# A perceiver layer on one core: the scores of the layer's own attention computed in two 64-row tiles of the TensorE array, with a PSUM bank for each

## The reference

```python
x = x + _L0_xattn_ref(_layernorm(x), ctx_1024, ctx_1024, ...)   # keys and values: 1601 rows a batch
x = x + _L0_attn_ref(_layernorm(x), ...)                        # the change is here
x = x + _L0_ffn_ref(_layernorm(x), ...)                         # 8 experts, the best 2 of a token

# _L0_attn_ref
qkv = jnp.einsum('bte,fe->btf', query, in_proj_weight).reshape(b, t, 3, H, D)
q = q / math.sqrt(D)
scores = jnp.einsum('bhqd,bhkd->bhqk', q, k)
scores = jnp.where(causal[None, None], scores, jnp.float32(-jnp.inf))
attn = jax.nn.softmax(scores, axis=-1)
out = jnp.einsum('bhqk,bhkd->bhqd', attn, v)
```

## Time and profile before

| | |
|---|---|
| median of 3 runs | 663.91 us (663.18 to 666.14) |
| profiled execution, its own time | 663.55 us |
| span of the profiled execution | 661.7 us |
| PE busy | 630.8 us, 95% |
| DVE busy | 475.3 us, 72% |
| ACT busy | 329.4 us, 50% |
| POOL busy | 301.9 us, 46% |
| chain that ended last | PE 74%, DVE 13% |
| mean granted TensorE clock | 0.989 |

### The profile page before, as it was taken

One profiled execution on the slowest core, in us unless ns is written; L12 is line 12 of the kernel. 1 busy time (PEld: TensorE's weight loads), 2 busy tenths in 40 slices (PEclk: granted clock), 3 DMA queues, 4 the chain that ended last, 5 costly groups with the idle time before them and its releaser, 6 DMA issues.

```text
span 661.7 us, 15583 instructions
## 1 busy us (share of the span) xinstructions
PE 630.8 (95%) x6304; PEld 532.8 (81%) x6312; DVE 475.3 (72%) x878; ACT 329.4 (50%) x541; POOL 301.9 (46%) x386
## 2 busy tenths in 40 slices
PE   7989999999989989989998999978989999999997
PEld 4778878868877868877887888757879999999997
DVE  4887757667687678688777868686777666656753
ACT  4355655555554555446555545463654444444421
POOL 2138788897686688678678768200000000000000
PEclk9999999999989999999999999998989999999999
DMA  6311110100010010011110000423003302330000
GB/s 184 134 50 52 28 51 26 51 27 26 27 52 1 27 50 27 26 27 51 27 27 26 2 1 2 152 106 127 1 1 128 128 26 104 127 127 0 0 0 33
DMA packets 13285, 34.11 MB, mean 52 GB/s; under 512 B 1563, under 2 KB 10532, under 8 KB 11044
## 3 DMA queue, kind: packets, MB, share of 16 engines
q1 hardware_dynamic: 13188, 33.19, 15.1%
q0 software_dynamic: 32, 0.01, 0.0%
HBM read 32.67 MB, written 0.52 MB: 50 GB/s over the span
## 4 chain that ended last, share of the span: by engine, by line
PE 74%; DVE 13%; issue 5%; ACT 3%; POOL 3%; DMA 2%; SPq 0%; POOLq 0%; DVEq 0%; ACTq 0%
PE bank L1207 46%; PE bank L1396 8%; PE bank L1216 7%; PE bank L1382 4%; PE bank L1277 3%; POOL prob_sum L490 3%; DVE maxes L923 3%; DVE ctx_lo L474 2%; DMA raw<-in_w 1%; ACT k_hi L626 1%; DVE k_lo L904 1%; PE bank L1332 1%; PE bank L1320 1%; PE bank L1304 1%; DVE prob_sum L490 1%
## 5 line engine op out<-in xcount | busy, mean ns | idle before, releaser
L490 POOL TENSOR_TENSOR prob_sum<-probs,prob_sum 128x256 f32<-128x256 f32 x336 | 270.6, 837 | 71.4 <-ACT probs L739 66.4
L739 ACT ACTIVATE probs<-bank 128x1024 f32<-128x1024 f32 (+1 forms) x104 | 106.6, 1025 | 111.6 <-PE bank L1396 99.2
L923 DVE TENSOR_REDUCE maxes<-bank 128x1 f32<-128x400 f32 (+1 forms) x256 | 129.5, 564 | 20.3 <-PE bank L1277 19.8
L721 ACT ACTIVATE h_raw<-bank,b_sb 128x512 f32<-128x512 f32 (+2 forms) x72 | 46.2, 642 | 106.5 <-PE bank L1207 106.3
L904 DVE SCALAR_TENSOR_TENSOR k_lo<-bank,bias_sb,k_hi 128x400 fp32r<-128x400 f32 (+2 forms) x64 | 40.5, 632 | 48.6 <-ACT k_hi L626 48.6
L1207 PE MATMUL bank<-w_hi,h_hi 128*128 128x256 f32 x256 | 73.6, 288 | 0.8 <-DVE h_lo L1142 0.8
L1207 PE MATMUL bank<-w_lo,h_hi 128*128 128x256 f32 x256 | 72.9, 285 | 0.0
L1207 PE MATMUL bank<-w_hi,h_lo 128*128 128x256 f32 x256 | 72.8, 284 | 0.0
L1216 PE MATMUL bank<-probs,v_sb 128*32 128x128 f32 (+1 forms) x1664 | 68.1, 282 | 1.0 <-ACT probs L739 0.5
L1141 DVE CAST h_hi<-h_raw 128x512 fp32r<-128x512 f32 (+2 forms) x72 | 28.5, 396 | 55.5 <-ACT h_raw L721 54.1
L1207 PE MATMUL bank<-wv_hi,ctx_hi 128*128 128x256 f32 (+1 forms) x208 | 65.3, 314 | 2.6 <-DVE maxes L923 2.4
(11 more groups left out here) (155 smaller groups left out, 1389.8 us busy)
## 6 DMA issues: line engine op xcount, KB each, us to landing
raw<-in_w SPq DMA_DIRECT2D x16, 1024.0 KB, 6.8
ctx_raw<-in_ctx_t SPq DMA_DIRECT2D x16, 400.0 KB, 3.6
ctx_raw<-in_ctx_t SPq DMA_DIRECT2D x8, 402.0 KB, 3.8
ctx_raw<-in_ctx_t SPq DMA_DIRECT2D x8, 399.0 KB, 3.6
w_sb<-in_w_t SPq DMA_DIRECT2D x1, 1280.0 KB
w_raw<-in_w_t SPq DMA_DIRECT2D x2, 256.0 KB, 4.7
result<-x_all SPq DMA_DIRECT2D x4, 128.0 KB, 2.0
x_all<-in_x SPq DMA_DIRECT2D x1, 384.0 KB, 4.1
```

Of the source, the lines that this page charges most:

```text
L490: ins = engine.tensor_tensor(prob_sum[0:ROWS[k], cols], probs[0:ROWS[k], s % 2, cols], acc[0:ROWS[k]], ALU.add)
L721: nc.scalar.activation(h_raw[:, c % 2, 0:width], bank[:, at, 0:width], ACT.Gelu, bias=b1_sb[:, bass.ds(e, 1), c:c + 1].rearrange("p a b -> ...
L739: nc.scalar.activation(probs[0:ROWS[k], s % 2, :].rearrange("p (g n) -> p g n", g=G), bank[0:ROWS[k], score_bank(b, k):score_bank(b, k) + ...
L923: nc.vector.tensor_reduce(maxes[:, g * PAIRS + j, c:c + 1], src[:, 0:width], AX.X, ALU.max).then_inc(read_dve, 1)
```

## The change

Own scores are computed in row tiles. Each of the 8 matmuls of `s0` and `s1` contracts over 64 rows in place of 128: the pairs of heads 0 and 1 of each group have their non-zero rows in rows 0 to 63, the pairs 2 and 3 in rows 64 to 127, so half of the 128 rows held zeros. Matmuls of the two row tiles alternate, and each row tile writes to a bank of its own. A piece `s0` is therefore two units, `("s0", 0)` and `("s0", 1)`; PE waits for both banks at once, then issues all 8 matmuls. DVE reads each bank with an instruction of its own, 256 elements a row in place of 512.

In a step these two units stand right behind the scores and the M units, ahead of K. In `CHAIN_AT` no K unit shares a step with `s0` or `s1`, so only step 7 of the last tile has another order. `GATE_BANKS` keeps `gt` and `b2` of the tail in the banks that they had, 3 and 6.

```diff
+GATE_BANKS = {"gt": 3, "b2": 6}
...
+        if banks is ALONE_BANKS:
+            for n, kind in enumerate(order):
+                self.bank[n] = GATE_BANKS.get(kind, self.bank[n])
...
-    others += [(c, 0) for c in chain]
-    row = m + others
+    others += [(c, 0) for c in chain if c not in ("s0", "s1")]
+    row = m + [(c, r) for c in chain if c in ("s0", "s1") for r in range(ROW_TILES)] + others
...
-                    nc.vector.tensor_tensor(soft[:, int(kind[1])], src.rearrange("p (n k) -> p n k", k=Q),
-                                            causal_sb[:, :].unsqueeze(1).broadcast_to([P, G * PAIRS, Q]),
+                    each = PAIRS // ROW_TILES
+                    nc.vector.tensor_tensor(soft[:, int(kind[1])].rearrange("p (g r i) q -> p r g i q", g=G, r=ROW_TILES)[:, u],
+                                            src[:, 0:G * each * Q].rearrange("p (g i q) -> p g i q", g=G, i=each),
+                                            causal_sb[:, :].unsqueeze(1).unsqueeze(1).broadcast_to([P, G, each, Q]),
...
-                    if kinds and kind not in kinds:
+                    if kinds and kind not in kinds or kind in ("s0", "s1") and u < ROW_TILES - 1:
...
-                    for g in range(G):
-                        for j in range(PAIRS):
-                            m = g * PAIRS + j
-                            ins = nc.tensor.matmul(dst[:, m * Q:m * Q + Q],
-                                                   own_queries[:, g, 2 * j:2 * j + 2, :].rearrange("p s q -> p (s q)"),
-                                                   k2_t[:, g, bi * Q:bi * Q + Q], start=True, stop=True)
+                    if u < ROW_TILES - 1:
+                        return
+                    each = PAIRS // ROW_TILES
+                    for g in range(G):
+                        for i in range(each):
+                            for r in range(ROW_TILES):
+                                rows, j = slice(RT * r, RT * r + RT), each * r + i
+                                at = (g * each + i) * Q
+                                ins = nc.tensor.matmul(bank[:, units.bank_of(n - ROW_TILES + 1 + r), at:at + Q],
+                                                       own_queries[rows, g, 2 * j:2 * j + 2, :].rearrange("p s q -> p (s q)"),
+                                                       k2_t[rows, g, bi * Q:bi * Q + Q], start=True, stop=True)
+                                if g == G - 1 and i == each - 1 and r < ROW_TILES - 1:
+                                    ins.then_inc(filled, 1)
```

More of the change, by code:

```diff
@@ L952, in after_units @@
             def after_units(units, s, *kinds):
-                for n, kind, _ in units.at[s]:
-                    if kinds and kind not in kinds:
+                for n, kind, u in units.at[s]:
+                    if kinds and kind not in kinds or kind in ("s0", "s1") and u < ROW_TILES - 1:
                         continue
@@ L1147, in alone @@
                     unit(TAIL, m, kind, u, TT - 1, B, 0)
-                    if kind == "s0":
+                    if kind == "s0" and u == ROW_TILES - 1:
                         after_units(TAIL, s, "s0")
```

## The result

The changed kernel takes 667.0 us (664.28 to 676.22, 20 executions), the kernel before on the same chip 663.23 us (659.46 to 671.58, 20 executions). The ratio is 1.0065 with a 95% interval of 1.004 to 1.009. Forecast were 662.7 us, a range of 661.0 to 666.2, and 0.84 for "no change": the time is outside the range, and it moved where no change was forecast. (Ratios here leave disturbed executions out, medians do not, so the two need not agree to the last digit.)

A forecast was written before the change was run, and what follows sets the result against it. PE is busy 95% of the span, but around these pieces the prediction took DVE to bound. Tile 1 -1.35, tile 2 +0.24, last tile +0.12 and tail +0.1 make -0.9 us: 663.55 to 662.7 us, range 661.0 to 666.2.

The forecast's parts named there:

- the emptier PE loses its clock: Rival: idle PE at step 8 of tiles 1 and 2 and in the tail lowers the clock; 666.2 us, chance 0.12.
- The new wait: Step 8, tiles 1 and 2: PE holds `s0` from 174.9 until 176.74, until DVE has read M unit 24's bank.
- What of it reaches the end: The part that sums the effects on tile 1, tile 2, the last tile and the tail to -0.9 us.
- V unit 6 late by 1.0 us: Step 8: `s0` ends at 177.65, so V unit 6 is about 1.0 us late, not 0.9 us early.
- Tile 1, -1.35 us: `t00` of tile 1 moves from 192.76 to 191.4, if the clock stays up.
- Tile 2, +0.24 us: `t00` of tile 2 already hangs on DVE, whose second reads for two pieces add 0.24 us.
- Last tile, +0.12 us: DVE's second read delays the division and `t00` of the last tile by 0.12 us.
- Ends: 0 and +0.5: The lower and upper bounds in us given for the last tile's delay.
- Tail, +0.1 us: In the tail the first read starts 0.15 us earlier and two reads cost 0.24, so +0.1 us.
- a gap of DVE between steps 8 and 11: A sign that the forecast is wrong: DVE, forecast to be without gaps there, has gaps between these steps.
- no pairs: Rival: float32 matmuls in different row tiles don't run together, a piece stays at 1.82 us; near 664.2 us, chance 0.10.
- PE's saving comes through: Rival: 8 pieces each 0.9 us shorter, nothing behind them held by DVE; 656.3 us, chance 0.10.

The follow-up runs named there:

- e3: The changed kernel with matmuls of ones filling PE's waits ahead of the own scores, in tiles 1, 2 and the last; 663.21 us, ratio 1.0001.
- e7: e4 with matmuls of ones in PE's waits ahead of the own scores and in the tail; 658.04 us, ratio 0.9938.
- e10: The kernel before with matmuls of ones ahead of `s1` in tiles 1 and 2 and in the tail, splits not moved; 660.22 us, ratio 0.9965.
- e6: The kernel before with each piece of own scores read by two instructions of 256 elements from its one bank; 662.81 us, ratio 0.9991.
- e1: The changed kernel without row tiles: 128 rows in each matmul, same two banks, reads and order; 670.11 us, ratio 1.0111.
- e11: e7 with own scores as matmuls of 128 rows into the same two banks; 662.08 us, ratio 1.0004.
- e5: The kernel before with two of the context splits one step later and nothing else; 662.93 us, ratio 1.0019.
- e2: The kernel before plus only a wait for DVE's read of M unit 24 (`s0`, tiles 1 and 2) or 28 (`s1`, last tile); 667.93 us, ratio 1.0112.
- e4: The changed kernel with two of the context splits one step later; 669.01 us, ratio 1.0039.

## Why the prediction was wrong

**The step that failed** is the clock behind the new wait. The prediction weighed it for tile 1 alone ("PE's gap ahead of `s1` falls to 0.8 us and `s1` to 0.9, so I expect that" it stays up), and in its terms for tile 2, +0.24 us, and for the last tile, +0.12 us, the clock stands at nothing. In tile 1 it did stay up. In tile 2, where it had not fallen before, and in the last tile it fell. They lost 2.23 and 2.03 us, and 0.55 and 0.46 in e3, where the same waits are filled: 1.7 and 1.6 us are the clock. In the medians, 3.5 us more at the lower clock are by the fit 1.6 us of the loss of 3.8 (the rest, from medians taken apart, is 2.4).

The third rival, "the emptier PE loses its clock", named this mechanism and came out at 666.2 us; its chance of 0.12 was far too small. That its number lies so near to 667.0 is in part luck: its places were wrong in part (tile 2 yes, the last tile in place of the tail), and it has no term for what was lost at full clock. Its condition, idle time beyond 1.77 us, was taken from a single execution: the changed kernel's 2.05 us in tile 2 fits it, 2.14 us in tile 1 and 1.45 in the last tile do not. The same code shows a mean clock of 0.972 to 0.991 from one execution to the next, so one trace can't tell a place where the clock is safe.

The Trainium skill, in "TensorE: Matmul & The Clock Gate", A second HAM failure mode: psum-queue depth-cycling, describes a kernel whose PE idles briefly between groups of matmuls as it goes round its banks, so that the clock swings between its levels. By this rule, the traces of tile 2 agree: 0.95 and then 0.63 behind a bank wait of 2.05 us, 1.00 with the same wait filled (e3); tile 1 doesn't, with 1.00 behind 2.14 us. The same page, HAM oscillation, counts half of the throttled time as lost; the runs show 0.44.

**The other 2.4 us are at full clock, from terms that were mis-sized** in "The new wait" and "What of it reaches the end". Single executions start apart by some tenths (the changed kernel's is 0.22 us late before the change begins), which is taken off here:

- *V unit 6 late by 1.0 us*: 1.43. The matmul was taken at 0.9 (1.04) and to start when M unit 24 is read; it starts 0.46 us after. The delay uses up the idle time at step 10, as I said, but more of it: 0.52 us are left, not 0.8. V unit 8 gains 0.55 us, near the 0.6 forecast.
- *Tile 1, -1.35 us*: at `t00` -1.66. At the end of the tile it is 0.45, because POOL's sums, 1.4 us late after step 8, took up all their gaps and ran longer. I had written that "POOL's sums of step 9 come 1.0 us later" and costed it at nothing. What was to hide them was idle time of POOL, and it was not enough. In e7, where `s0` comes in time, nothing is lost between `t00` and the end of the batch. Nor was the term a gain of the change alone: e10, without row tiles, shortens tile 1 by 1.25 us, because the clock stays up there. Most of the 1.35 us was the fall of the clock in the one execution that I read.
- *Tile 2, +0.24 us*: +0.99 at `t00` (303.79 against 303.03, in an execution that was 0.23 us early by then), and +2.23 at the end of the tile, by the clock and POOL. With the clock up (e3) it is +0.55.
- *Last tile, +0.12 us, "Ends: 0 and +0.5"*: +2.03, and +0.46 in e3. `s1` was to start at 401.9 for 401.29. It started at 404.70; less the 1.96 us that the tile was late already, that is 1.45 us of new delay and not 0.6. K's reading on DVE stands at 398.37 in place of 394.62, 1.8 us later by the same correction (1.5 forecast), and the maxima behind it inherit that.
- *Tail, +0.1 us*: nearly right, once the clock is taken out. `t00` waits 1.18 us for DVE (1.9 forecast), `t10` 0.52 as before.

**What held**: eight rounds in pairs (1.04 us, 0.9 forecast); the idle time ahead of `s0`, released by DVE's maxima; `t00` behind DVE; two reads at 0.76 us for 0.68 (+0.08, +0.12 forecast, and e6 shows no cost); PE's busy time down by 4.4 us (7.3 forecast) and the span not. One of its signs of being wrong came true, a gap of DVE between steps 8 and 11: 1.13 us in tile 2, behind the fallen clock. The rival "no pairs" fell in the trace itself, and "PE's saving comes through" fell with the wait: e1 and e11 put the row tiles' own saving at 3.1 and 4.0 us (2.9 and 3.2 at full clock) for six hidden pieces and two of the tail, not 7.3.

**What stays open.** How the loss divides between clock and wait is bounded, not fixed: at full clock 2.4 us by the fit for the unfilled pair, 1.6 in the token tiles of the profiled e3 and e10, and only 0.3 by the fit for that filled pair, a difference within its scatter. How much of it is the wait and how much the order of the last tile was not taken apart. The place at which the clock falls next was seen to move between kernels, and no run says why it fell in tile 2 and not in tile 1, with 2.05 and 2.14 us of idle time. A fall in tile 2 isn't proof of the bank wait by itself: e5, which has no such wait, fell there too (0.58 in 294 to 298).

## What to carry to other kernels

Work saved on the busiest engine can be worth nothing if it asks for one more buffer than is free: look first at who empties that bank, and at what stands ahead of it in that engine's queue (here 1.52 us of a split that could as well come one step later). On PE a wait can be paid twice, once as idle time and again as lower clock behind it (here 1.6 to 1.7 us for each fall); judge such a change from granted clocks of many executions, and test it with filled waits, for the kernel before as well, since a gain of 3 us may lie in the filling alone, and fill both in the same places. A term that is hidden by another engine's idle time (POOL's here) needs the length of that idle time beside it.

## What the runs showed of the hardware that was not expected

- A microsecond at the lower clock cost 0.44 us of the span over 192 executions, nearly the whole half, though PE is "only" 95% busy. Matmuls of ones in PE's waits bought 3.0 us for the kernel before (0.9965, interval 0.9953 to 0.9977).
- Float32 matmuls of 64 rows and 64 columns in two row tiles do run together: 8 rounds in 1.04 us.
- From the end of the read that frees the bank to the first matmul some 0.46 us passed in tile 1 (an estimate: the read is the first of four equal ones that take 2.00 us together). The same matmuls behind one bank's wait (e2) stood idle 1.83 us, behind the two-bank code (e1) 2.05 us.
  The Trainium skill, in "Perfetto Trace Analysis", Identifying Dependency Chains, says that an instruction that waits for several engines may have EventSemaphore instructions with further conditions put ahead of it. No run here counts them, and `s0` waits for the same engines in e2 and in e1, so they don't explain the 0.22 us between these two.
- Once fallen, the clock can stay low while PE works: 0.50 to 0.53 in each 4 us from 484 to 508 in e4, with PE busy for 3.35 to 4.00 of them.
- The clock fell also in places that no kernel here changed, such as the tail's first chunks: this line of the changed kernel stands for them.

```profile
453.00:457.00 4.00, 3.29 (x23) 2.87 (x24) 2.69 (x5) 0.01 (x1) 0.00 (x0) 0.57 0.82 285
```
